# A masked-softmax graph layer on one core: one of the scores' two cross products is computed, the other comes as its transpose over HBM

## What is computed

```
u      = h h^T / sqrt(384)                     # 256 x 256, symmetric
delta  = softmax(u, rows) * adjacency
attn   = delta / (row sum of delta + 1e-10)
ctx    = upper(attn) (h W_left^T + b_left) + diag(attn) * (h W_self^T + b_self)
         + lower(attn) (h W_right^T + b_right)
y      = h + relu(layernorm(ctx, 1e-12) * gamma + beta)
out    = layernorm(y, 1e-5)
```

## Time and profile before

| what | us |
|---|---|
| median of 3 runs | 504.95 |
| lowest and highest run | 504.54, 506.44 |
| the profiled execution, its own time | 508.25 |
| its span in the trace | 506.5 |
| TensorE busy | 479.6 (95%), 2902 matmuls |
| VectorE busy | 339.9 (67%) |
| ScalarE busy | 334.3 (66%) |
| GpSimd busy | 220.6 (44%) |
| HBM traffic over the span | 130 GB/s |

### The profile page before, as it was taken

The page is one execution under the profiler, slowest core; times in us unless marked ns, Lnnn a source line. Parts: engine busy times, 40 slices in busy tenths (PEclk is TensorE's granted clock), DMA queues, the critical chain, the costliest instruction groups (busy, mean ns, idle before and its releaser), DMA issues.

```text
span 506.5 us, 9515 instructions
## 1 busy us (share of the span) xinstructions
PE 479.6 (95%) x2902; PEld 477.7 (94%) x2902; DVE 339.9 (67%) x876; ACT 334.3 (66%) x740; POOL 220.6 (44%) x297
## 2 busy tenths in 40 slices
PE   7579999999999999999999999999999999999980
PEld 7579999999999999999999999999999999999970
DVE  2447766777776667777666777766677777667652
ACT  3356576767667776776676677667666866767642
POOL 0215543344554334455533445554334555433454
PEclk9889999999999999999999999999999999999995
DMA  8560344433444443344444334444433344442201
GB/s 246 179 208 26 112 145 155 134 102 121 142 149 135 155 145 93 122 139 143 135 155 155 107 113 130 137 135 155 155 114 115 123 137 142 148 156 74 72 32 62
DMA packets 63889, 65.90 MB, mean 130 GB/s; under 512 B 4736, under 2 KB 59776, under 8 KB 63872
## 3 DMA queue, kind: packets, MB, share of 16 engines
q1 hardware_dynamic: 63872, 65.69, 40.6%
HBM read 44.70 MB, written 20.97 MB: 130 GB/s over the span
## 4 chain that ended last, share of the span: by engine, by line
PE 91%; DMA 3%; DVE 1%; ACT 1%; POOL 1%; SPq 1%; issue 1%; POOLq 0%; ACTq 0%; DVEq 0%
PE ps_proj L299 58%; PE ps_ctx L335 20%; PE ps_scores L299 13%; DMA w_raw<-in_L_gnn_W_right 2%; DMA dt_raw<-dt_dram 1%; POOL shifted L670 0%; DMA dt_dram<-turned 0%; POOL scaled L666 0%; DVE w_lo L564 0%; SPq L259 0%; SPq L251 0%; ACT w_hi L434 0%; POOLq L99 0%; ACT ps_scores L373 0%; POOL rstd L662 0%
## 5 line engine op out<-in xcount | busy, mean ns | idle before, releaser
L299 PE MATMUL ps_proj<-w_hi,xt_hi 128*128 128x384 f32 x576 | 194.4, 337 | 6.9 <-DVE w_lo L564 4.1
L299 PE MATMUL ps_proj<-w_lo,xt_hi 128*128 128x384 f32 x576 | 194.2, 337 | 0.0
L299 PE MATMUL ps_proj<-w_hi,xt_lo 128*128 128x384 f32 x576 | 194.2, 337 | 0.0
L662 POOL TENSOR_TENSOR rstd<-var_eps,minus_half 128x4 f32<-128x4 f32 x33 | 33.6, 1018 | 217.8 <-DVE var_eps L536 216.0
L391 ACT ACTIVATE proj_hi<-ps_proj 128x384 fp32r<-128x384 f32 x128 | 62.6, 490 | 90.1 <-PE ps_proj L299 90.1
L299 PEld LDWEIGHTS ps_proj<-w_hi,xt_hi 128*128 128x128 f32 x576 | 108.7, 189 | 7.7 <-DVE w_lo L564 4.4
L387 ACT ACTIVATE ps_proj<-bias 128x384 f32<-128x384 f32 (+1 forms) x192 | 94.1, 492 | 29.8 <-DVE proj_lo L506 26.4
L299 PEld LDWEIGHTS ps_proj<-w_hi,xt_lo 128*128 128x128 f32 x576 | 108.7, 189 | 0.0
L299 PEld LDWEIGHTS ps_proj<-w_lo,xt_hi 128*128 128x128 f32 x576 | 108.7, 189 | 0.0
L506 DVE TENSOR_TENSOR proj_lo<-ps_proj,proj_hi 128x384 fp32r<-128x384 f32 x128 | 67.2, 544 | 59.1 <-ACT proj_hi L391 59.1
L666 POOL TENSOR_TENSOR scaled<-normed,gamma_sb 128x384 f32<-128x384 f32 x64 | 64.7, 1011 | 36.4 <-ACT normed L409 36.4
(11 more groups left out here) (61 smaller groups left out, 717.3 us busy)
## 6 DMA issues: line engine op xcount, KB each, us to landing
xt_sb<-in_x_t SPq DMA_DIRECT2D x32, 384.0 KB, 3.8
x_sb<-in_x SPq DMA_DIRECT2D x32, 384.0 KB, 4.4
out_dram<-out_sb SPq DMA_DIRECT2D x32, 384.0 KB, 2.7
adj_sb<-in_adj SPq DMA_DIRECT2D x32, 256.0 KB, 4.4
dt_dram<-turned SPq DMA_DIRECT2D x32, 256.0 KB, 2.0
dt_raw<-dt_dram SPq DMA_DIRECT2D x128, 64.0 KB, 2.0
w_raw<-in_L_gnn_W_left SPq DMA_DIRECT2D x1, 576.0 KB, 4.3
w_raw<-in_L_gnn_W_right SPq DMA_DIRECT2D x1, 576.0 KB, 9.8
```

The source lines that it names most:

```text
L299: mm = nc.tensor.matmul(to, stationary, moving, start=(k == 0 and not seeded), stop=(k == len(passes) - 1), skip_group_check=seeded)
L662: nc.gpsimd.tensor_tensor(rstd[at.slot(2)][:], var_eps[:], minus_half[:], ALU.pow).then_inc(rstd_ready, 1)
```

## The change

TensorE computes the high by high product and only one of the two cross products. The other is its transpose. So `cross` computes one cross product two batches ahead, VectorE transposes its blocks out of PSUM (`turn_cross`), SP stores it and loads it back, and `squares`, a step later, adds high by high in the same PSUM bank. VectorE adds both in `finish_scores`, scales by -1/sqrt(384) and takes the row's least value in the same instruction, which replaces `maxima` and ScalarE's `neg_max`. The columns of the scores stand in another order (`keys`), in runs of 32. There are two banks of scores. `xt` is loaded and split a batch earlier. The orders of the engines change, and batch 0 has one of its own, with the whole product for its own scores.

```diff
 # SP
+            def store_cross(at):
+                sp.wait_ge(cross_turned_ready, at.n(1, 0))
+                sp.dma_start(cross_dram[:], cross_turned[:]).then_inc(cross_stored, 16)
+            def load_cross(at):
+                sp.wait_ge(cross_stored, at.n(16, 0))
+                for q in range(Q):
+                    sp.dma_start(cross_raw[q * R:(q + 1) * R]...., cross_rows[q]).then_inc(cross_loaded, 16)
...
             def one(at):
...
+                if at.plus(-3).exists(BATCHES):
+                    store(at.plus(-3))
+                    load_xt(third.n(1), third.slot(UNROLL))
+                    load(ahead.n(1), ahead.slot(UNROLL))
                 if nxt.exists(BATCHES):
-                    turn(nxt)
-                if behind.exists(BATCHES):
-                    store(behind)
+                    store_turned(nxt)
+                if ahead.exists(BATCHES):
+                    store_cross(ahead)
+                if nxt.exists(BATCHES):
+                    load_turned(nxt)
+                if ahead.exists(BATCHES):
+                    load_cross(ahead)
 # TensorE
+            def keys(tile):
+                return tile.rearrange("p (h q c) -> p q h c", q=Q, c=R)
+            def cross(at):
+                pe.wait_ge(xt_lo_ready, at.n(1, 1))
+                if at.b != 1:
+                    pe.wait_ge(delta_ready, at.n(T, -T))
+                for t in range(T):
+                    for c in range(C):
+                        mm = nc.tensor.matmul(ps_scores[at.slot(2)][:, t, :], xt(at, c, t * P, (t + 1) * P)[0], keys(xt(at, c, 0, L)[1]),
+                                              start=(t == 0 and c == 0), stop=(c == C - 1), skip_group_check=True)
+                mm.then_inc(cross_ready, 1)
+            def squares(at):
+                pe.wait_ge(cross_turned_ready, at.n(1, 0))
+                for t in range(T):
+                    for c in range(C):
+                        mm = nc.tensor.matmul(ps_scores[at.slot(2)][:, t, :], xt(at, c, t * P, (t + 1) * P)[0], keys(xt(at, c, 0, L)[0]),
+                                              start=False, stop=(c == C - 1), skip_group_check=True)
                 mm.then_inc(scores_ready, 1)
...
             def one(at):
-                nxt = at.plus(1)
-                project(at, 0)
-                project(at, 1)
-                if nxt.exists(BATCHES):
-                    scores(nxt)
-                for g in range(2, NG):
+                nxt, ahead = at.plus(1), at.plus(2)
+                if at.b != 0 and nxt.exists(BATCHES):
+                    squares(nxt)
+                for g in range(NG):
                     project(at, g)
+                    if at.b == 0 and g == 3:
+                        cross(nxt)
+                    if at.b == 0 and g == 4:
+                        squares(nxt)
+                    if g == 4 and ahead.exists(BATCHES):
+                        cross(ahead)
 # ScalarE
                 split_proj(at, 0)
-                split_delta(at)
                 if before.exists(BATCHES):
                     normalise(before)
+                split_delta(at)
                 split_proj(at, 1)
                 seed_proj(at, 4)
-                seed_proj(at, 5)
-                if nxt.exists(BATCHES):
+                if at.b == 0:
+                    split_proj(at, 2)
+                    split_proj(at, 3)
+                    seed_proj(at, 5)
                     exps(nxt)
-                split_proj(at, 2)
-                split_proj(at, 3)
+                else:
+                    if nxt.exists(BATCHES):
+                        exps(nxt)
+                    split_proj(at, 2)
+                    seed_proj(at, 5)
+                    split_proj(at, 3)
                 if nxt.exists(BATCHES):
                     seed_proj(nxt, 0)
                 seed_ctx(at, 0)
 # VectorE
+            def turn_cross(at):
+                dve.wait_ge(cross_ready, at.n(1, 0))
+                if at.b != 1:
+                    dve.wait_ge(cross_stored, at.n(16, -16))
+                nc.vector.transpose(cross_turned[:]...., ps_scores[at.slot(2)][:]....).then_inc(cross_turned_ready, 1)
-            def maxima(at):
+            def finish_scores(at):
+                if at.b != 0:
+                    dve.wait_ge(cross_loaded, at.n(64, 0))
                 dve.wait_ge(scores_ready, at.n(1, 1))
-                nc.vector.reduce_max(row_max[:], ps_scores[:], AX).then_inc(row_max_ready, 1)
+                nc.vector.memset(gate[:], 0.0)
+                for t in range(T):
...
+                    nc.vector.tensor_tensor_reduce(ps, ps, other, -SCALE, LARGEST, ALU.add, ALU.min, neg_max[:, t:t + 1]
+                                                   ).then_inc(neg_max_ready, 1)
             def deltas(at):
...
-                nc.vector.tensor_tensor(delta[:], ps_scores[:], adj_sb[at.slot(UNROLL)][:], ALU.mult).then_inc(delta_ready, 1)
+                for t in range(T):
...
+                    nc.vector.tensor_tensor(d, ps_scores[at.slot(2)][:, t, :]...., a, ALU.mult).then_inc(delta_ready, 1)
...
             def one(at):
...
                     norm_shift(before)
-                split_delta(at)
-                split_proj(at, 1)
-                if nxt.exists(BATCHES):
-                    maxima(nxt)
-                if before.exists(BATCHES):
+                if at.b == 0:
+                    split_delta(at)
+                    for g in range(1, NSPLIT):
+                        split_proj(at, g)
+                    turn_cross(nxt)
+                    finish_scores(nxt)
+                    deltas(nxt)
+                    turn(nxt)
+                else:
+                    if nxt.exists(BATCHES):
+                        finish_scores(nxt)
+                    split_delta(at)
+                    split_proj(at, 1)
                     residual(before, 0)
                     residual_stats(before, 0)
-                if nxt.exists(BATCHES):
-                    deltas(nxt)
-                    turn(nxt)
-                split_proj(at, 2)
-                split_proj(at, 3)
+                    if nxt.exists(BATCHES):
+                        deltas(nxt)
+                        turn(nxt)
+                    split_proj(at, 2)
+                    split_proj(at, 3)
+                if ahead.exists(BATCHES):
+                    turn_cross(ahead)
                 if nxt.exists(BATCHES):
                     diagonal(nxt)
```

More of the change, by code:

```diff
@@ L158, in gnn_resnorm @@
         shifted = sb("shifted", [P, T, H])
-        ps_scores = psum("ps_scores", [P, T, L])
-        ps_warm = psum("ps_warm", [P, P])
+        ps_scores = [psum(f"ps_scores{i}", [P, T, L]) for i in range(2)]
         ps_proj = [psum(f"ps_proj{i}", [P, BANK]) for i in range(PBANKS)]
@@ L233, in gnn_resnorm @@
         dt_dram = nc.dram_tensor("dt_dram", [P, Q * T * T * R], F32, kind="Internal")
-        dt_rows = dt_dram.rearrange("(a c) (q e) -> q c a e", c=R, q=Q)
+        cross_dram = nc.dram_tensor("cross_dram", [P, Q * T * T * R], F32, kind="Internal")
+        dt_rows, cross_rows = (d.rearrange("(a c) (q e) -> q c a e", c=R, q=Q) for d in (dt_dram, cross_dram))
         block = ctx.enter_context(nc.Block())
@@ L260, in _ @@
                     sp.dma_start(adj_sb[0][:], adj_rows[0]).then_inc(adj_loaded[0], 16)
-                    sp.dma_start(xt_sb[1][:], xt_rows[1]).then_inc(xt_loaded[1], 16)
+                    load_xt(1, 1)
             for to, vector in ((gamma_sb, gamma), (beta_sb, beta)):
                 sp.dma_start(to[:], vector.partition_broadcast(P)).then_inc(vectors_loaded, 16)
[L264 to L269, removed]
+            load_xt(2, 2)
+            sp.dma_start(x_sb[0][:], x_rows[0]).then_inc(x_loaded[0], 16)
+            load(1, 1)
+            first = Batch(0, 0)
+            store_turned(first)
+            load_turned(first)
+            store_cross(first.plus(1))
+            load_cross(first.plus(1))
             def store(at):
@@ L275, in one @@
             def one(at):
-                ahead, behind, nxt = at.plus(2), at.plus(-2), at.plus(1)
-                if behind.exists(BATCHES):
-                    if ahead.exists(BATCHES):
-                        sp.wait_ge(y_ready, behind.n(T, T))
-                        load(ahead.n(1), ahead.slot(UNROLL))
-                if nxt.exists(BATCHES):
-                    turn(nxt)
-                if behind.exists(BATCHES):
-                    store(behind)
+                nxt, ahead, third = at.plus(1), at.plus(2), at.plus(3)
+                if at.plus(-3).exists(BATCHES):
+                    store(at.plus(-3))
+                if third.exists(BATCHES):
+                    if at.plus(-1).exists(BATCHES):
+                        sp.wait_ge(xt_lo_ready, at.n(1, 0))
+                    load_xt(third.n(1), third.slot(UNROLL))
+                if ahead.exists(BATCHES):
+                    if at.plus(-2).exists(BATCHES):
+                        sp.wait_ge(y_ready, at.n(T, -T))
```

(38 more changed lines are left out.)

52 lines of the change are left out of this document (36 added, 16 removed).

## The result

The changed kernel is slower. Its median is 531.54 us (531.11 to 535.03, 4 runs) beside 505.69 of the kernel before; the ratio is 1.0532, 95% interval 1.0508 to 1.0556. The 505.69 is the median of four executions of which one, at 1685.59, was a slow one and has no part in the ratio; the other three took 504.54 to 506.44, median 504.95 as before. The prediction was 526, range 509 to 533.

The account below looks back on a forecast made before the run. TensorE bounds the kernel, but a second chain with 0.76 us slack would take over: thirty batches +17.1 and the start +3.9 make +21.0, added to the median 504.95 for 526 us, range 509 to 533.

Parts of the forecast that it names:

- The second chain: ScalarE `proj_hi` through VectorE and GpSimd to `seed_ctx` and first `attend`: 8.99 us, slack 0.76; becomes the bound, late by 0.66.
- The collision, +0.48: VectorE's later `split_delta` meets GpSimd's beta 0; they take turns, and `residual(…, 0)` ends at 5.91 instead of 5.43 us.
- the sum: Adding up the chain's links in one batch from moment 0, projection group 0 ready for ScalarE; `attend` at 9.53 us.
- The sum's 0.86 for beta 0: GpSimd's beta 0, after `split_delta` holds until 3.65, then needs 0.86 us and ends at 4.52 instead of 4.04.
- The operand in runs of 32: TensorE's moving operand read in 32-column runs: cost between nothing and a doubling (0.71 us of `squares`); taken as nothing.
- `finish_scores` is covered: On VectorE between `norm_shift` and `split_delta`: 0.7 to 1.4 us in a hole of 1.06 to 2.96, costing nothing.
- The trip hides: Cross product's store and load over HBM: lands at 15.1 to 16.2 us, wanted at 16.3; 512 KB more per batch hide.
- VectorE has room behind `turn_cross`: `turn_cross`, about 0.71 us, stands off the chain behind `split_proj` 3; 0.3 us or more remain before the next `context_stats`.
- The batch, 15.26: Steady batch: `attend` at 9.53, then both `attend`, `squares` and group 0; 15.25 to 15.26 us, +0.57, thirty batches +17.1.
- +0.06 for a second `deltas`: VectorE's `deltas` as two operations of 256 instead of one of 512: 0 to 0.14 us for a second start, +0.06 taken.
- The start, +3.9: Batch 0's `seed_ctx` waits for the cross product's trip: first `attend` 36.8 instead of 33.39, +0.5 for clock; bounds 0 and +6.
- The clock in the steady batches: TensorE standstills of 1.2 us per batch leave the clock up; a fall, strided operand and late load together: chance 0.09.

Follow-up runs that it names:

- experiment 4: Changed kernel with `squares` behind projection group 1 instead of ahead of group 0: median 515.70 us, ratio 1.0223 to the kernel before.
- experiment 5: Changed kernel with ScalarE's and VectorE's orders around `split_delta` set back and `squares` behind projection group 1: median 496.25 us, ratio 0.9821 to the kernel before.
- experiment 1: Changed kernel with ScalarE's `split_delta` ahead of `normalise` and VectorE's ahead of `finish_scores` again, `squares` left: median 518.72 us, ratio 1.0263 to the kernel before.
- Experiment 2: Changed kernel, orders kept, VectorE's `split_delta` reading its second operand from unused, zeroed PSUM instead of SBUF: median 517.18 us, ratio 1.0241 to the kernel before.
- experiment 7: Changed kernel without `store_cross`, `load_cross` and their waits, `finish_scores` adding zeros: median 525.68 us, ratio 1.0409 to the kernel before.
- experiment 8: Changed kernel with `turn_cross` done twice, the first time into a tile nobody reads: median 532.78 us, ratio 1.0539 to the kernel before.
- experiment 9: Kernel before the change with only ScalarE's `split_delta` moved behind `normalise`: median 505.50 us beside 505.20, ratio 1.0005.
- experiment 3: Changed kernel with only ScalarE's order around `split_delta` set back, VectorE's `finish_scores` still ahead of it: median 529.23 us, ratio 1.0481 to the kernel before.

## Why the prediction was right, point by point

- **The second chain becomes the bound: shown.** The chain of the kernel after runs through it, and moving `squares` back gives 0.68 a batch where VectorE starts first (experiment 4) and 0.73 where there is no collision (experiment 5 against experiment 1, 14.87 to 14.14).
- **The collision, +0.48: shown.** 15.35 less the 14.87 of experiments 1 and 2 is 0.48. Beta 0 at 1.50, and `seed_proj(nxt, 0)` at 8.49 (283.00 after 274.51), where the sum had 8.47. By the Trainium skill, page SBUF — State Buffer, section Who interferes with whom, a VectorE instruction with two inputs in SBUF contends with a GpSimd instruction that reads SBUF, and the first to issue makes the other wait. The traces agree in both directions of the race (beta 0 at 1.50 beside `split_delta` at 0.69, and 1.02 beside 1.46), and for a `TENSOR_TENSOR`, which no row of before showed. By the same section a VectorE instruction with at most one input in SBUF does not contend. Experiment 2 agrees: 0.69 and 1.03. The prediction called the 0.27 that `affine_select` still took after `residual` the streaming time of its columns. That is not shown. Beside an idle VectorE the same operation takes 0.40, and what fits all the meetings is simpler: the one that waited ends its own length less 0.13 to 0.15 after the other. The sum's 0.86 for beta 0 fits it.
- **The operand in runs of 32: nothing,** `squares` takes 0.71 for 6 matmuls, the same 0.119 each. **`finish_scores` is covered:** two operations of 0.45 in the hole. **The trip hides:** experiment 7. **VectorE has room behind `turn_cross`:** experiment 8.
- **The batch, 15.26: 15.21 to 15.24 in the batches written out ahead of and behind the loop, about 15.35 in the loop.** Up to `seed_proj(nxt, 0)` the sum is right to 0.02, the +0.06 for a second `deltas` included (0.87 from `deltas` to `turn`, 280.94 to 281.81, for 0.80). The terms that were too small are the small ones behind it: TensorE started 0.67 after `seed_ctx` and not 0.63 as in batch 0, which makes 0.04, and from there to ScalarE's start on the next group 0 it took 5.75 (284.10 to 289.85) and not 5.72, with 0.10 for the restart instead of 0.08. The hand-over from batch 0 was the wrong one to take, because the same hand-overs are shorter outside the loop: 0.64 for 0.67, and 0.77 from `deltas` to `turn` (66.13 to 66.90) for 0.87; the kernel before has 0.71 (45.93 to 46.64) for 0.80. These two are the 0.13 between the batches outside and within. Why they are longer in the loop was not tried. Over the batches it makes about 2 us, the 529.5 − 527.5.
- **The start, +3.9: the place was right, the size partly.** The first `attend` was 3.8 late (3.4 predicted), behind a standstill of 4.05 (some 5 predicted). But the profiled execution of the kernel before was itself slowed at that place, a standstill of 1.88 and a clock of 0.52 behind it, its first batch taking 16.39. In experiment 9, with the same order on TensorE, it was 0.79 and 14.79, and the execution took 504.73 instead of 508.25. If the other executions of before were like this, as their median of 505 suggests, the start loses 3.5 us more against them than against the profiled one. With the 2 us of the batches this is the gap between the predicted 526 and the measured 531.5. That step failed, though the range held the result: the difference of two spans was added to the median, though the profiled execution was 3.3 above it, and the slow start stood in the rows. What made it slow is open.
- **The clock in the steady batches: right.** A standstill of about 1 us in each (1.2 predicted) left it at 1.00.

So it is not the removed product that failed to pay. It gave its 0.71 a batch (experiment 5 has it, less 0.16 of standstill and restart), and 1.2 were lost beside it: 0.71 to the place where half of it was put, 0.48 to an order of two queues.

## What to carry to other kernels

Before work is taken off the bounding engine, measure how far the next chain is behind, and ask of what remains whether it stands inside or outside that chain: here 0.71 us of matmuls ahead of a projection cost as much as the same 0.71 had saved. A reordering on one engine moves what another engine runs later; look at what GpSimd does at the new time, when the moved VectorE operation has two inputs in SBUF. And when a median is predicted from a profiled execution, ask first what in it was out of the ordinary.

## What the runs showed of the hardware

- Which of VectorE and GpSimd starts first decides who waits. VectorE held with a lead of 0.02 us (experiment 4) to 0.13 (experiment 3), GpSimd with one of 0.11 or more. In three batches of experiment 4 in which the starts lay within 0.01 of each other VectorE held (beta 0 took 1.56 or 1.57).
- The one that waits then needs less than its whole length, by 0.13 to 0.15: a GpSimd operation of 1.02 us ended 0.88 after VectorE's, one of 0.40 (`affine_select`) ended 0.27 after, a VectorE operation of 0.56 ended 0.41 after GpSimd's, one of 0.69 ended 0.55 after (experiment 4).
- The addition with scale and minimum runs as a custom operation: 0.43 to 0.47 us for 256 columns and 0.14 for reading the result; a 512-column transpose out of PSUM takes 0.70, one out of SBUF 0.71.
- TensorE's clock fell after a standstill of 1.88 that followed another of 1.18, and stayed up through 30 standstills, one in each batch, 29 of about 1 us and the last of 1.71. The length of one standstill alone does not decide it: in the kernel of experiment 5 one of 2.25 left it at 1.00 in the stretch behind it.

```profile
26.99 0.41 PE L337 MATMUL ps_proj<-w_hi,xt_hi 128*128 128x384 f32 x1 [2.25 <-ACT ps_proj L451]
```

```profile
27.00:35.00 8.00, 5.08 (x30) 4.44 (x30) 1.94 (x5) 1.02 (x3) 1.42 (x4) 1.00 0.29 92
```
